# Copying the transposed u straight out of PSUM, and reordering it in the gate's fp32 matmul instead

## The chip, the cores and the metric

The kernel runs on one core of one Trainium2 chip. The metric is the device time of one launch in microseconds. The time before is 427.67 us, the median of three runs (427.49 to 428.02).

## What is computed

An image `x` of 16 batches, 32 x 32 places and 32 channels goes through three residual layers. The first is an upsampling and downsampling filter with a leaky ReLU; the second is causal self-attention over the 1024 places of a batch; the third is a mixture of 16 experts, and it is this one that the change touches:

```python
t = t + attention(layernorm(t))              # t: 16 batches x 1024 tokens x 32
u = layernorm(t)
logits = einsum('bsd,ed->bse', u, gate_w) + gate_b
probs = softmax(logits, axis=1)              # over the 1024 tokens of a batch
vals, idx = top_k(probs.transpose(0, 2, 1), 8)   # each expert takes 8 tokens of each batch
pooled = sum over the 8 tokens of u[token] * probs[token]
out = gelu([pooled, 1] @ weight1) @ weight2      # per expert
t[token] += out * probs[token]
```

## The kernel before

The 16 batches are worked through one after the other, and everything that concerns the gate is done for four batches at once (a group; G = 4 groups). The order of the work is a list written by hand, `EVENTS`, which every engine walks through: an engine executes the events that concern it and leaves the others out, so one list sets the order of each of the five queues. In the middle of the kernel the list interleaves stages of several batches (`STEP`); the last group's gate and the experts' work come in the order of `LAST` (L140 to L143).

The stages of the gate for group n are these. "uT" on TensorE (L973) turns the normalised tokens `u` with eight fp32 transposes into two PSUM banks of psA, 128 partitions (four batches times 32 channels) by 1024 tokens. "uT" on VectorE (L752) copies these 1024 columns into the SBUF tile `uT`. The columns come as (a, r, q) with a of 2, r of 4 and q of 128, and they are written as (a, q, r): VectorE reads PSUM in order and writes every fourth place of `uT` (16 bytes apart), four times 128 places for each half. After this a token stands at its own number. "logits" on TensorE (L976) waits for that copy and multiplies the block-diagonal gate matrix `gateT` (128 x 64) by the 1024 columns of `uT`, in two fp32 products of 512 columns. ScalarE then adds the bias and copies the 64 x 1024 logits to `lg` (L564), VectorE looks for the eight largest (L755, L759), ScalarE makes the exponential and the scaling (L568, L572), VectorE masks the rest (L764), and TensorE turns the weights back ("wT", L980), reading `xF_all` through `by_tile`, every fourth column as the stationary operand. "pool" (L983) and the experts ("hidden", "experts", "turned", "scatter") follow.

The program writes one product of fp32 operands; the trace shows two pairs of a weight load and a matmul for each, so the two products of a group are four MATMULs of 128 x 512 (a transpose is one pair).

The same tile `uT` is also called `att`: "proj" on VectorE (L720) writes into it before "mean" adds it to `t2_all`, and it waits until the last group's logits are in `lg` (L721). In front of the next group's `att` nothing else reads `uT`.

In the middle of the kernel "uT" is followed on VectorE by work on other batches ("low", "down", "shift", "score"), and on TensorE between "uT" and "logits" lie "down", "shift", "zV", "prob" and "score" of other batches. In `LAST` TensorE finds between ("uT", 3) and ("logits", 3) the event ("experts", 0): 32 small products of `hid` with `w2_sb` (L999).

Of the kernel before, what the change touches and what calls it, by code (L numbers as in the profile page):

```python
# [17 lines left out]
R = P // C  # L18
# [16 lines left out]
GE = GB * E_  # L35
# [5 lines left out]
BANK = 512  # L41
# [152 lines left out]
def hybrid_kernel(nc, x, bias, up_filter, dn_filter, Wq, Wk, Wv, gate_w, gate_b, weight1, weight2, out):  # L194
# [8 lines left out]
    with ExitStack() as ctx:  # L203
# [3 lines left out]
        def sem(name):  # L207
            return ctx.enter_context(nc.semaphore(name))
# [41 lines left out]
        uT = sb("uT", [P, S])  # L250
# [25 lines left out]
        gateT = sb("gateT", [P, GB, E_])  # L276
# [52 lines left out]
        a_filled, a_drained = sem("a_filled"), sem("a_drained")  # L329
# [251 lines left out]
        def _(dve):  # L581
# [19 lines left out]
            for e in EVENTS:  # L601
# [3 lines left out]
                s = slot(e) if e in A else None  # L605
                if name == "xT":
                    nc.vector.tensor_copy(xF_all[:, n, :], s).then_inc(a_drained, 1)
                    dve.wait_ge(a_drained, A[e] + 1)
                    for b in range(GB):
                        link(nc.vector.bn_stats(stats[:, :], xF_all[:, n, BC * b:BC * b + BC]))  # L610
                        ins = nc.vector.bn_aggr(mv[:, n, b, :], stats[:, :])
# [11 lines left out]
                elif name == "normalise":  # L623
                    dve.wait_ge(g_rstd, nth("gn_var", n))
                    for b in range(GB):
                        r = slice(BC * b, BC * b + BC)
                        ins = nc.vector.tensor_scalar(x_all[:, n, r], xF_all[:, n, r], gmean[:, n, b:b + 1], grstd[:, n, b:b + 1],
                                                      ALU.subtract, ALU.mult)
# [13 lines left out]
                elif name == "UU":  # L642
                    dve.wait_ge(fills_ready, 4)
                    dve.wait_ge(U_split, 2)
                    for r in range(R):
                        q = slice(C * r, C * r + C)
# [23 lines left out]
                elif name == "dnT":  # L670
# [4 lines left out]
                    for r in range(R):  # L675
                        ins = nc.vector.tensor_copy(DD[:, :, r:r + NS, r, :], D_parts[:, :, :, :])
# [13 lines left out]
                elif name == "split_z":  # L690
                    s = centred[:, :].rearrange("p (n c) -> p n c", c=C)
# [13 lines left out]
                elif name == "score":  # L705
                    if n >= 2:
                        dve.wait_ge(a_filled, A["shift", n - 2] + 1)
                    for m, at in packed(e[2]):
                        ins = nc.vector.tensor_reduce(negmax[:, n % 2, m - 1:m], s[:, at:at + P * m], X, ALU.max, negate=True)  # L709
# [40 lines left out]
                        dve.wait_ge(t2_rstd, 2 * G)  # L750
                        nc.vector.tensor_tensor(pair_of_u(e[2]), pair_of_u(e[2]), per_token(urstd[:, :]), ALU.mult).then_inc(u_ready, 1)
                elif name == "uT":  # L752
                    nc.vector.tensor_copy(uT[:, :].rearrange("p (a q r) -> p a r q", a=2, r=R),
                                          s.rearrange("p (a r q) -> p a r q", a=2, r=R)).then_inc(a_drained, 1)
                elif name == "logit_max":  # L755
                    dve.wait_ge(b_drained, BU["logits", n] + 1)
                    link(nc.vector.max(top8[:, :], lg[:, :]))
# [28 lines left out]
                elif name == "pool":  # L786
                    for b in range(GB):
                        ins = nc.vector.tensor_copy(pooled32[:, :, b], s[C * b:C * b + C, E_ * b:E_ * b + E_])
# [12 lines left out]
                elif name == "turned":  # L801
                    groups = range(PARTS[n][0] // GB, PARTS[n][1] // GB)
                    for g in groups:
                        ins = nc.vector.tensor_tensor(obd[:, g, :, :], s[0:GE, C * g:C * g + C].unsqueeze(1).broadcast_to([GE, GB, C]),
                                                      blocks(GB, C, GE, C_BDE), ALU.mult)
                    ins.then_inc(a_drained, 1)
                elif name == "scatter":
                    for a in range(2):
# [3 lines left out]
                        else:  # L812
                            dve.wait_ge(a_filled, A[e] + 1)
                        ins = nc.vector.tensor_tensor(x_all[:, n, :].rearrange("p (b k c) -> p k b c", b=GB, k=KT)[:, tiles],
                                                      s.rearrange("p (k b c) -> p k b c", b=GB, k=KT)[:, tiles],
                                                      t2_all[:, n, :].rearrange("p (b k c) -> p k b c", b=GB, k=KT)[:, tiles], ALU.add)
# [3 lines left out]
        def _(pe):  # L820
# [32 lines left out]
            for e in EVENTS:  # L853
# [4 lines left out]
                s = slot(e) if e in A or e in BU else None  # L858
                if name == "xT":
                    pe.wait_ge(x_loaded[n], 16)  # L860
                    ins = turn(s, lambda k: x_all[:, n, P * k:P * k + P], ident)
                elif name == "gn_mean":
                    pe.wait_ge(stats_ready, nth("xT", n))
                    ins = nc.tensor.matmul(s[:, 0:GB], cst[:, C_AVG:C_AVG + P], mv[:, n, :, 0], start=True, stop=True)
                elif name == "gn_var":
                    pe.wait_ge(a_drained, A["gn_mean", n] + 1)
                    ins = nc.tensor.matmul(s[:, 0:GB], cst[:, C_AVG:C_AVG + P], gvar[:, n, :], start=True, stop=True)
                elif name == "small" and n == 0:
# [3 lines left out]
                    ins = nc.tensor.matmul(s[:, BANK:BANK + E_], gw_sb[:, :, :], ident[0:E_, 0:E_], start=True, stop=True)  # L872
                elif name == "small" and n == 1:
                    pe.wait_ge(a_drained, A["small", 0] + 1)
                    nc.tensor.matmul(s[0:C, 0:C], A_sb[:, :], cst[0:C, C_Q:C_Q + C], start=True, stop=True)
                    ins = nc.tensor.matmul(s[:, BANK:BANK + C], cst[0:C, C_QREP:C_QREP + P], wvT[:, :], start=True, stop=True)
                elif name == "small":
                    pe.wait_ge(a_drained, A["small", 1] + 1)
                    ins = nc.tensor.matmul(s[:, 0:C], T1[:, :, :], cst[0:C, C_Q:C_Q + C], start=True, stop=True)
                elif name == "dnT":  # L880
                    pe.wait_ge(dn_toeplitz_loaded, 16)
                    rows = dnE.rearrange("p a t -> p (a t)")
                    for m in range(NS):
                        ins = nc.tensor.matmul(s[:, C * m:C * m + C], rows[:, 2 * W * (2 * m + 1):2 * W * (2 * m + 3)], ident[0:C, 0:C],
                                               start=True, stop=True)
# [18 lines left out]
                elif name == "tok":  # L904
# [3 lines left out]
                    for k in range(HB):  # L908
                        ins = nc.tensor.matmul(s[:, BC + P * k:BC + P * k + P], image_cols(n, k), cst[:, C_Q:C_Q + P], start=True, stop=True)
# [41 lines left out]
                elif name == "pv":  # L951

                    pe.wait_ge(b_drained, BU["zV", n] + 1)
                    waited = set()
                    for j in range(KT):
                        unit = next(u_ for u_ in range(NU) if KT - j in PACK[u_])
                        if unit not in waited:
                            waited.add(unit)
                            pe.wait_ge(*low_count(n, unit))
                        o, N = PLACE[j], P * (KT - j)  # L960
                        for part in range(2):
                            probs_j = Pp[:, n % 2, part, o:o + N].rearrange("p (t r q) -> p t r q", r=2, q=2 * C)
                            for odd in range(2):
                                rows = s[2 * C * odd:2 * C * odd + 2 * C, :].rearrange("p (r t q) -> p t r q", r=2, t=KT)[:, j:KT]
                                ins = nc.tensor.matmul(rows, zV[:, n % 3, j, :], probs_j[:, :, :, C * odd:C * odd + C],  # L965
                                                       start=j == 0 and part == 0, stop=j == KT - 1 and part == 1, skip_group_check=True)
                elif name == "proj":
                    pe.wait_ge(b_drained, BU["pv", GB * n + 2 * e[2] + 1] + 1)
                    for k in range(KT):
                        b, a, r = k // 4, k // 2 % 2, k % 2  # L970
                        at = S // 4 * r + P * a
                        ins = nc.tensor.matmul(s[:, P * k:P * k + 2 * C + 2], oT[:, 2 * e[2] + b, at:at + P], V2[:, :], start=True, stop=True)  # L972
                elif name == "uT":  # L973
                    pe.wait_ge(u_ready, 2 * n + 2)
                    ins = turn(s, lambda k: u[:, k, :], ident)
                elif name == "logits":  # L976
                    pe.wait_ge(a_drained, A["uT", n] + 1)
                    for i in range(2):
                        ins = nc.tensor.matmul(s[0:GE, BANK * i:BANK * i + BANK], gateT[:, :, :], uT[:, BANK * i:BANK * i + BANK], start=True, stop=True)  # L979
                elif name == "wT":  # L980
                    pe.wait_ge(route_ready, n + 1)
                    ins = turn(s, by_tile(xF_all[0:GE, n, :]), ident[0:GE, 0:GE], GE)
                elif name == "pool":  # L983
                    pe.wait_ge(a_drained, A["wT", n] + 1)
                    for k in range(KT):
                        ins = nc.tensor.matmul(s[:, 0:GE], u[:, k, :], wT[:, k, :], start=k == 0, stop=k == KT - 1)
                elif name == "hidden":
                    first, last = PARTS[n]
                    if n == 0:
                        pe.wait_ge(w1_split, 2)  # L990
                    pe.wait_ge(pooled_split, 2 * (last // GB))
                    for x_ in range(E_):
                        ins = nc.tensor.matmul(s[:, B * x_ + first:B * x_ + last], w1_parts[:, x_, :], pooled[:, x_, first:last], start=True, stop=True)
                elif name == "experts":
                    first, last = PARTS[n]
                    pe.wait_ge(b_drained, BU["hidden", n] + 1)
                    sv = s[0:C, 0:B * E_].rearrange("p (b e) -> p e b", b=B)[:, :, first:last]
                    for x_ in range(E_):
                        ins = nc.tensor.matmul(sv[:, x_, :], w2_sb[:, x_, :], hid[:, x_, first:last], start=True, stop=True)  # L999
                elif name == "turned":  # L1000
                    pe.wait_ge(a_drained, A["experts", n] + 1)
                    for g in range(PARTS[n][0] // GB, PARTS[n][1] // GB):
                        ins = nc.tensor.transpose(s[0:GE, C * g:C * g + C], o2[:, GB * g:GB * g + GB, :], ident[0:C, 0:C])
                elif name == "scatter":
                    pe.wait_ge(a_drained, A["turned", n // (G - 1)] + 1)
                    tile = by_tile(xF_all[0:GE, n, :])
                    for k in range(KT):
                        ins = nc.tensor.matmul(s[:, P * k:P * k + P], tile(k), obd[:, n, :, :], start=True, stop=True)  # L1008
                        if k == R - 1:
                            ins.then_inc(half_filled, 1)  # L1010
                else:
                    continue
# [26 lines left out]
```

## Time and profile before

| | |
|---|---|
| median of three runs | 427.67 us |
| profiled execution, its own time | 429.69 us |
| its span on the core | 427.8 us |
| TensorE matmuls, busy | 356.7 us, 83% |
| VectorE busy | 323.8 us, 76% |
| ScalarE busy | 257.0 us, 60% |
| GpSimd busy | 238.3 us, 56% |
| granted TensorE clock, mean | 0.892 |

The profile is of one execution. Its span is the time from the first to the last instruction on the core; 1.89 us of its own time lie outside that span. Busy shares are means over the whole span, and the stages differ: up to about 340 us the four engines all work at once, from 390 us on only TensorE, VectorE and ScalarE take turns, at half of TensorE's clock. A group of instructions is named by its line, engine, and output <- inputs, and a MATMUL names the moving operand first, the stationary operand second. "idle before <- X" is the time for which the engine stood still before the group, and X is what ended it. A matmul's own duration includes the way through the array, which overlaps the next one; the pace of a series is read from the starts, or from the length of the whole series over its count.

### The profile page before, as it was taken

To read this page: it belongs to the slowest core of one execution; us is meant where nothing else is said; L and a number is where in the kernel's file an instruction comes from. 1 tells how busy PE (TensorE), PEld (TensorE's weight loads), DVE (VectorE), ACT (ScalarE), POOL (GpSimd) and SP (SyncE) were. 2 spreads that over 40 slices of the span, in tenths; PEclk is the share of its full clock that TensorE was granted. 3 is DMA by queue.
4 is the path that set the end of the run, shared out by engine and by line. 5 is a ranking of instruction groups with operands and counts; after the bars stand their busy time and mean duration, and the time that the engine had idled before them with its cause. 6 is when DMAs were issued, how large, how long until landed. Compare 5 with 4: busy or idle time off the path is not lost.

```text
span 427.8 us, 7761 instructions
## 1 busy us (share of the span) xinstructions
PE 356.7 (83%) x3022; PEld 267.0 (62%) x3022; DVE 323.8 (76%) x551; ACT 257.0 (60%) x342; POOL 238.3 (56%) x138
## 2 busy tenths in 40 slices
PE   1199899999999997989988979898788697854995
PEld 1088777677778584748766847486654345443785
DVE  3878957887778778987787789777979888773631
ACT  0122424788998867589766675997485856811500
POOL 5405543485895996774755967747558735132000
PEclk9999979999999998999998989999898886855555
DMA  4700000000000000000000000000410000000122
GB/s 110 180 1 2 0 2 2 2 3 1 3 2 2 2 2 1 2 2 0 2 2 2 0 3 0 2 2 2 90 13 2 1 0 2 2 0 0 51 73 75
DMA packets 16432, 6.82 MB, mean 16 GB/s; under 512 B 6479, under 2 KB 16269, under 8 KB 16397
## 3 DMA queue, kind: packets, MB, share of 16 engines
q1 hardware_dynamic: 13680, 5.68, 5.7%
q10 hardware_dynamic: 2717, 0.66, 0.9%
q8 instruction: 24, 0.39, 0.4%
q14 instruction: 11, 0.09, 0.1%
HBM read 4.16 MB, written 2.11 MB: 15 GB/s over the span
## 4 chain that ended last, share of the span: by engine, by line
PE 55%; DVE 18%; issue 9%; ACT 9%; DMA 3%; POOL 2%; SPq 1%; POOLq 1%; ACTq 1%; DVEq 0%
PE psB L839 10%; PE psA L839 9%; PE psB L965 5%; PE psB L947 5%; PE psA L932 4%; DVE negmax L709 4%; PE psA L1008 4%; PE psA L972 3%; ACT e L552 3%; ACT Pp L553 3%; PE psB L979 3%; DVE Pp L376 2%; PE psA L829 2%; DVE t_all L734 2%; PE psA L925 2%
## 5 line engine op out<-in xcount | busy, mean ns | idle before, releaser
L376 POOL TENSOR_TENSOR Pp<-e,Pp 128x1024 f16<-128x1024 f32 x45 | 99.1, 2203 | 30.8 <-ACT Pp L553 30.6
L709 DVE TENSOR_REDUCE negmax<-psA 128x1 f32<-128x512 f32 (+7 forms) x128 | 91.0, 750 | 21.2 <-PE psA L935 20.8
L552 ACT ACTIVATE e<-psB 128x1024 f32<-128x1024 f32 (+1 forms) x80 | 76.1, 951 | 11.0 <-PE psB L947 8.6
L553 ACT ACTIVATE Pp<-psB 128x1024 f16<-128x1024 f32 (+1 forms) x80 | 76.7, 958 | 0.0
L839 PE MATMUL psB<-xin,UU 128*128 128x224 f16 (+1 forms) x480 | 60.1, 287 | 2.1 <-ACT oT L557 1.8
L947 PE MATMUL psB<-yQ,zK 128*128 128x512 f16 (+1 forms) x192 | 51.6, 347 | 7.4 <-ACT Pp L553 4.6
L839 PE MATMUL psA<-y,DD 128*128 128x224 f16 (+1 forms) x480 | 55.2, 273 | 1.5 <-DVE negmax L709 1.5
L839 PEld LDWEIGHTS psB<-xin,UU 128*128 128x128 f16 x480 | 49.1, 103 | 11.0 <-ACT oT L557 2.1
L932 PE MATMUL psA<-zK,yQ 128*128 128x512 f16 x192 | 47.7, 337 | 7.2 <-DVE tF L682 5.7
L839 PEld LDWEIGHTS psA<-y,DD 128*128 128x128 f16 x480 | 46.6, 98 | 7.2 <-DVE negmax L709 1.9
L441 POOL TENSOR_TENSOR zrstd<-zrstd,power 128x8 f32<-128x8 f32 x16 | 30.8, 1924 | 30.4 <-DVE zrstd L689 30.1
L463 POOL TENSOR_TENSOR y<-y 128x1024 f16<-128x1024 f32 x16 | 37.9, 2371 | 17.2 <-ACT y L518 17.2
L965 PE MATMUL psB<-Pp,zV 128*64 128x128 f16 (+7 forms) x512 | 38.7, 299 | 8.1 <-DVE Pp L376 7.9
L376 DVE TENSOR_TENSOR Pp<-e,Pp 128x1024 f16<-128x1024 f32 (+1 forms) x35 | 40.9, 1176 | 0.9 <-ACT Pp L553 0.7
L965 PEld LDWEIGHTS psB<-Pp,zV 128*64 128x64 f16 x512 | 24.6, 114 | 24.9 <-DVE Pp L376 12.1
L515 ACT ACTIVATE y<-psB 128x1024 f16<-128x1024 f32 x16 | 16.4, 1023 | 33.4 <-PE psB L839 33.4
L947 PEld LDWEIGHTS psB<-yQ,zK 128*128 128x128 f16 x192 | 17.5, 102 | 24.4 <-ACT Pp L553 9.1
L441 POOL TENSOR_TENSOR urstd<-urstd,power 128x16 f32<-128x16 f32 x8 | 23.2, 2894 | 12.9 <-DVE urstd L748 12.9
L704 DVE TENSOR_TENSOR yQ<-psA,yQ 64x1024 f16<-64x1024 f32 x16 | 19.6, 1228 | 13.6 <-ACT yQ L541 13.5
L932 PEld LDWEIGHTS psA<-zK,yQ 128*128 128x128 f16 x192 | 17.2, 101 | 20.3 <-DVE tF L682 6.3
L950 PE MATMUL psB<-ident_b,mask_b 128*128 128x128 bf16 x128 | 29.2, 228 | 0.0
L471 POOL COPY z<-z 128x512 f16<-128x512 f16 x16 | 12.8, 803 | 25.3 <-DVE z L700 25.3
(154 smaller groups left out, 626.4 us busy)
## 6 DMA issues: line engine op xcount, KB each, us to landing
x_all<-in_x_dram SPq DMA_DIRECT2D x4, 512.0 KB, 4.7
out_dram<-x_all SPq DMA_DIRECT2D x8, 256.0 KB, 2.3
y<-in_L_ffn_weight_dram SPq DMA_DIRECT2D x3, 256.0 KB, 4.2
yQ<-rows SPq DMA_DIRECT2D x32, 2.0 KB
Pp<-filter_tables ACTq DMA_DIRECT2D x4, 121.9 KB, 3.1
cst<-shape_constants SPq DMA_DIRECT2D x1, 326.5 KB, 4.3
xin<-in_L_ffn_weight_dram SPq DMA_DIRECT2D x1, 256.0 KB, 4.8
Pp<-filter_tables ACTq DMA_DIRECT2D x1, 120.0 KB, 3.3
```

The source lines that it names most:

```text
L376: return engine.tensor_tensor(Pp[:, n % 2, 1, o:o + N], e32[:, (NU * n + i) % 3, 0:N], Pp[:, n % 2, 0, o:o + N], ALU.subtract)
L441: return nc.gpsimd.tensor_tensor(v, v, power[:, 0:1].broadcast_to([P, n]), ALU.pow)
L463: nc.gpsimd.tensor_tensor(low, y32[:, :], high, ALU.subtract).then_inc(y_ready, 1)
L552: nc.scalar.activation(e32[:, m % 3, 0:N], slot(e)[:, 0:N], ACT.Exp)
L553: nc.scalar.activation(Pp[:, n % 2, 0, UOFF[e[2]]:UOFF[e[2]] + N], slot(e)[:, 0:N], ACT.Exp).then_inc(b_drained, 1)
L704: nc.vector.tensor_tensor(v, s[2 * C:P, :], v, ALU.subtract).then_inc(a_drained, 1)
L709: ins = nc.vector.tensor_reduce(negmax[:, n % 2, m - 1:m], s[:, at:at + P * m], X, ALU.max, negate=True)
L839: ins = nc.tensor.matmul(within(out_cols, -shift), m, within(v, shift), start=i == 0, stop=i == len(matrices) - 1)
L932: ins = nc.tensor.matmul(s[:, lo:hi], yQ[:, n % 3, P * (m - 1):P * m], zK[:, n % 3, lo - at:hi - at], start=True, stop=not diagonal)
L947: ins = nc.tensor.matmul(s[:, lo:hi], zK[:, n % 3, P * j:P * j + P], yQ[:, n % 3, P * j + lo - at:P * j + hi - at], start=True, stop=not d ...
L950: ins = nc.tensor.matmul(s[:, lo:lo + P], mask_b[:, :], ident_b[:, :], start=False, stop=True)
L965: ins = nc.tensor.matmul(rows, zV[:, n % 3, j, :], probs_j[:, :, :, C * odd:C * odd + C], start=j == 0 and part == 0, stop=j == KT - 1 and ...
```

## The change

VectorE copies the 1024 columns of PSUM into `uT` in the order in which they stand, (a, r, q). Each of the two products of "logits" then reads its 512 columns of `uT` in the order (q, r): r is the inner step. So the output columns stand in the order of the tokens as before, and `lg` and all behind it is unchanged. Going by the access pattern, one column and the next are 128 fp32 values (512 bytes) apart in groups of four, and each group of four begins one place (4 bytes) behind the last; "four places apart", as the change is called in words, is the spacing of the writes that it removes. The number of instructions, their sizes, the waits and the order of the events stay the same.

```diff
                 elif name == "uT":
-                    nc.vector.tensor_copy(uT[:, :].rearrange("p (a q r) -> p a r q", a=2, r=R),
-                                          s.rearrange("p (a r q) -> p a r q", a=2, r=R)).then_inc(a_drained, 1)
+                    nc.vector.tensor_copy(uT[:, :], s).then_inc(a_drained, 1)
...
                 elif name == "logits":
                     pe.wait_ge(a_drained, A["uT", n] + 1)
                     for i in range(2):
-                        ins = nc.tensor.matmul(s[0:GE, BANK * i:BANK * i + BANK], gateT[:, :, :], uT[:, BANK * i:BANK * i + BANK], start=True, stop=True)
+                        ins = nc.tensor.matmul(s[0:GE, BANK * i:BANK * i + BANK], gateT[:, :, :], uT[:, BANK * i:BANK * i + BANK].rearrange("p (r q) -> p q r", r=R), start=True, stop=True)
```

## Rows read from the trace of the kernel before

**Rows 1.** Table by stage: stretch, busy us (instructions) per engine, PEclk, DMA share, GB/s.

```profile
60.00:176.00 116.00, 110.34 (x1041) 83.28 (x1040) 89.53 (x151) 89.74 (x122) 84.36 (x49) 0.99 0.01 2
...
390.00:427.80 37.80, 30.76 (x184) 26.42 (x184) 14.75 (x30) 6.29 (x7) 0.00 (x0) 0.50 0.20 56
```

**Rows 2.** The chain that ended last, in time: start us, us, engine, line.

```profile
176.96 3.46 PE psA L839 x30
181.79 1.86 PE psB L979 x4
185.85 1.02 ACT zK L531
...
267.41 1.86 PE psB L979 x4
...
341.98 3.68 PE psB L979 x4
...
392.27 1.97 DVE uT L753
394.38 3.64 PE psB L979 x4
```

**Rows 3.** The lines L753 and L607: VectorE copies, ns min/median/max, first and last start.

```profile
L753 DVE COPY uT<-psA x4: 1958/2006/2014, 176.8 to 392.3; 128x1024 f32<-128x1024 f32 x4
L607 DVE COPY xF_all<-psA x4: 1215/1222/1226, 7.6 to 41.9; 128x1024 f32<-128x1024 f32 x4
```

**Rows 4.** Timeline of the end: start, us, engine, line, operation, [idle before <- releaser].

```profile
392.17 1.88 PE L999 MATMUL psA<-hid,xin 128*32 128x12 f32 x32
392.27 1.96 DVE L753 COPY uT<-psA 128x1024 f32<-128x1024 f32 x1 [2.12 <-PE psA L829]
394.09 0.35 DVE L799 TENSOR_TENSOR o<-psA,w2bias 32x192 f32<-32x192 f32 x1
...
394.38 3.64 PE L979 MATMUL psB<-uT,gateT 128*64 128x512 f32 x4 [0.33 <-DVE uT L753]
```

**Rows 5.** Timeline about the first of the four copies.

```profile
176.82 2.01 DVE L753 COPY uT<-psA 128x1024 f32<-128x1024 f32 x1
...
181.34 0.41 DVE L682 SCALAR_TENSOR_TENSOR tF<-psA,xF_all 128x256 f32<-128x256 f32 x1
...
181.72 1.93 PE L979 MATMUL psB<-uT,gateT 128*64 128x512 f32 x4
...
183.58 0.55 PE L932 MATMUL psA<-zK,yQ 128*128 128x512 f16 x2
...
184.34 1.29 DVE L709 TENSOR_REDUCE negmax<-psA 128x1 f32<-128x896 f32 x2 [1.48 <-PE psA L935]
```

**Rows 6.** Timeline about the third copy.

```profile
338.04 2.00 DVE L753 COPY uT<-psA 128x1024 f32<-128x1024 f32 x1 [0.48 <-PE psA L829]
...
341.98 3.68 PE L979 MATMUL psB<-uT,gateT 128*64 128x512 f32 x4 [1.50 <-ACT Pp L553]
...
346.35 2.48 DVE L709 TENSOR_REDUCE negmax<-psA 128x1 f32<-128x896 f32 x4 [1.14 <-PE psA L935]
```

**Rows 7.** Table by stretch, columns as in rows 1: the clock during the gate's products.

```profile
181.00:184.00 3.00, 3.00 (x14) 1.07 (x13) 1.82 (x5) 2.75 (x4) 2.85 (x2) 1.00 0.00 1
341.00:346.00 5.00, 4.02 (x7) 0.98 (x8) 4.17 (x5) 1.23 (x3) 2.12 (x1) 0.54 0.00 1
394.00:398.00 4.00, 3.67 (x6) 0.79 (x6) 0.43 (x2) 0.00 (x0) 0.00 (x0) 0.50 0.00 0
```

**Rows 8.** Timeline: transposes with a stationary operand in order and with a spaced one.

```profile
175.25 1.04 PE L829 MATMUL psA<-cst,u 128*128 128x128 f32 x8
...
206.62 1.17 PE L829 MATMUL psA<-cst,xF_all 64*128 64x64 f32 x8
...
207.73 0.39 PE L947 MATMUL psB<-yQ,zK 128*128 128x512 f16 x1
```

**Rows 9.** The chain in time, at half clock: the same transposes with the spaced operand.

```profile
361.38 1.15 PE psA L829 x8
```

## The prediction

> **What bounds the kernel now.** I read the table by stage first. From 60 to 176 us TensorE is busy for 110.34 of 116.00 us at a granted clock of 0.99, and it stays the fullest engine up to about 340 us; in the last 37.80 us it is busy for 30.76, at clock 0.50 [rows 1]. So the middle is paced by TensorE, with VectorE close behind, and the end is a chain in which the engines take turns. The reader should see that the change takes time from VectorE and can only add time to TensorE.
>
> Next I read the chain that ended last, in order of time, for the four groups. The copy L753 stands in it once, at the end (392.27, 1.97 us). In the middle the chain passes beside it: near the first group it goes from the convolution L839 (176.96) through the gate's products L979 (181.79, 1.86 us) to ScalarE's zK (185.85), and at the later place through L979 again (341.98, 3.68 us) [rows 2]. So there are four copies of which one counts, and four sets of products which all count. Two early sets, at 181.79 and 267.41, take 1.86 us each; the clock at the first was 1.00 and the second repeats it. The sets at 341.98 and 394.38 ran at 0.54 and 0.50, that is at 1.2 GHz [rows 7].
>
> **The copy.** What is left is a plain copy of 128 x 1024 fp32 from PSUM to SBUF. The trace of before holds exactly this form: L607, 1222 ns. The reordering copy takes 2006 ns, so each copy becomes 0.78 us shorter (the last one, 1958 ns, becomes 0.74 us shorter) [rows 3]. The sum over four is 3.1 us of VectorE.
>
> How much of it is on the path? At the end, TensorE does the 32 small products of the experts, 392.17 to 394.05, while VectorE copies, 392.27 to 394.23; the gate's products begin at 394.38, after an idle time of 0.33 us that the copy ended [rows 4]. With the copy done at 393.49, the experts' products end last, and the gate can begin at 394.05 plus almost nothing. So the cover of those 1.88 us leaves a gain of 0.33 us out of 0.74. What is late next is TensorE itself. The experts' addition L799 can't begin before the experts' products end, and it begins at 394.09 already [rows 4], so nothing else moves up. All that follows the gate hangs on L979 (the chain goes from the copy into it [rows 2]) and moves with it.
>
> In the middle I take the copy's gain as zero. After the copy at 176.82, VectorE has L376 and then L682 (181.34); these would come some 0.7 us earlier. But TensorE is busy without a gap from the products at 181.72 into L932 at 183.58, so no wait for VectorE stands there, and the next thing VectorE does after that, L709 at 184.34, waited 1.48 us for TensorE already [rows 5]. The 0.78 us become a longer wait there. The group at 338.04 is the same: the gate waited for ScalarE (1.50 us, Pp L553), not for the copy, and VectorE then waited 1.14 us for TensorE before L709 at 346.35 [rows 6]. If the cover were gone in all three places the gain would be 3 x 0.78 = 2.3 us more; that is a rival below.
>
> **The gate's products.** No row of before shows a moving operand read with its columns 512 bytes apart, so this cost has to be bounded. Before: four MATMULs from 181.72 to 183.58 [rows 5], which is 465 ns for each 512 columns or 0.91 ns per column at full clock; at half clock 3.64 / 4 = 910 ns, 1.78 ns per column [rows 4].
>
> The lower bound is no cost: the instruction needs a new fp32 value only every 0.91 ns, which a read may still keep up with. A gain is excluded, since the counts and the sizes stay the same, and an instruction that read in order already can't be read faster.
>
> The nearest row on TensorE is the weight load of "wT", which reads 128 fp32 values 16 bytes apart. Eight of its transposes take from 206.62 to 207.73, 139 ns each, at full clock; eight transposes whose operand is read in order, and which stream twice as many columns, take 1.04 us or 130 ns each [rows 8]. At half clock the spaced ones take 1.15 us, 144 ns each [rows 9]. Half the work in no less time, and a pace that hardly moves when the clock halves: I read this as a limit in the read and not in the array, 139 / 128 = 1.09 ns for each fp32 value that is read apart from its neighbours. Applied to the moving operand, 512 x 1.09 = 556 ns in place of 465 at full clock, so 91 ns more for each MATMUL, 0.36 us for a set of four and 0.73 us for the two sets at full clock. At half clock 556 ns lie below the 910 ns that the array takes, and nothing is added.
>
> The farther row is VectorE's own spaced write: (2006 - 1222) / 1024 = 0.77 ns more for each value [rows 3]. Put upon the measured plain pace of 1.09 ns/value as the cost of going from line to line, it is 1.86 ns, or 952 ns for 512 columns: 487 ns more for a MATMUL at full clock, 42 ns more at half clock. That is 8 x 0.487 + 8 x 0.042 = 4.2 us. The upper bound is the limit of 1.09 ns with every column read twice, once for each of two sweeps of the array: 1112 ns, or 647 more at full and 202 more at half clock, 8 x 0.647 + 8 x 0.202 = 6.8 us. I take 1.09 ns once, since it is the row on the same engine and of the same type of data.
>
> The rows of the spaced write and of the spaced weight load both show a cost for 16 bytes already [rows 3, 8]. The Trainium skill, in "SBUF — State Buffer" (the note on SBUF cachelines), says that reads are at full rate as long as at least two fall on the same line of 16 bytes, and that a stride of up to four fp32 values is free; past that every access pays. The new reads are far past that and speak against the change; the old write at 16 bytes cost 0.77 ns a value in this trace, so here the trace does not bear out that four are free. The page gives no price, so the sum stays as it is.
>
> **The sum.** Products +0.73, copy at the end -0.33, copies in the middle 0: +0.40 us. The profiled execution took 429.69 us with a span of 427.8, 2.02 us above the median of 427.67 us; the change in the span carries over to the median: 428.07, rounded to 428.1 us.
>
> **Why the products' cost is passed on.** TensorE goes from L979 straight into L932 at 183.58, whose scores VectorE was waiting for (1.48 us) [rows 5], and the chain leads on from L979 to zK [rows 2]. There is no slack behind the products in the middle that would take up 0.36 us.
>
> **The rivals.** The measurement of this kernel can tell about 0.2% (0.86 us) from no change: below 426.8 is faster, over 428.5 slower.
>
> Rival A: the moving read keeps up, because a column is wanted only every 0.91 ns. For it speaks that the needed pace is only a sixth below the 1.09 ns limit and that this port need not have the weight port's limit; against it the spaced weight loads [rows 8]. Only the end's 0.33 us are left: 427.3 us, not to be told from no change.
>
> Rival B, slower: going from line to line costs TensorE's moving port more than its weight port, from the 952 ns to the 1112 ns above, or four values 512 bytes apart fall on the same part of the memory. Its place is the eight MATMULs at full clock. The price is 4.2 - 0.33 = +3.9 us, 431.5 us, up to 6.8 - 0.33 = +6.5, 434.1 us. It decides once it costs 1.19 us (0.86 + 0.33), which is 149 ns per MATMUL at full clock: 614 ns, 1.20 ns per column. For it speaks VectorE's 0.77 ns [rows 3]; against it, that TensorE's weight port took 1.09 ns in all.
>
> Rival C, faster: VectorE's 0.78 us reach the path in some of the three places of the middle as well, since VectorE there is nearly as full as TensorE (89.53 of 116.00 us [rows 1]). All three with rival A give 427.67 - 0.33 - 2.3 = 425.0 us, one or two of them 426 to 426.5. Against it are the waits of 1.48 and 1.14 us in which VectorE stood still right afterwards [rows 5, 6].
>
> That the change doesn't do what it says (the copy stays at 2.0 us) is nearly excluded by L607, the same form [rows 3]: 428.4 us then.
>
> **How the numbers follow.** The forecast (428.1) has 0.36, rival A (427.3) 0.24, rival B (431.5 to 434.1) 0.28, rival C (425.0 to 426.5) 0.11, the last one 0.01. The range of 426.5 to 432.0 holds the forecast, A, the cheaper part of B (0.17 of 0.28) and the edge of C (0.03): 0.80. Faster: C, 0.11. Slower: B and a tenth of the forecast, whose 91 ns per MATMUL need only be 149: 0.32. Same: 0.57.
>
> **What would show it right or wrong.** In the profile after, L753 should stand at 1222 ns four times. At the end L979's idle time before should fall from 0.33 us to near 0, ended by L999 and not by the copy. The four MATMULs of L979 near 181 us should take about 2.2 us from start to start of what follows, where it was 1.86; those near 342 and 394 us should be unchanged at 3.6 us. VectorE's wait before L709 near 184 us should grow from 1.48 us to over 2. The forecast is wrong if the sets at half clock also become longer (then the read is slower than 1.78 ns per column, rival B), or if the span shortens before 390 us (rival C), or if TensorE's clock falls in another stretch because its work has moved.

## The result

The changed kernel takes 432.57 us (median of 14 runs, 428.9 to 434.5), where the kernel before took 427.94 us in the 14 runs beside it (425.44 to 432.74). The ratio is 1.010 with an interval of 1.0065 to 1.0135, that is 2.8 to 5.8 us slower. A second series gave 1.0067 (1.0035 to 1.0099). The single executions of one and the same kernel lie over 7 us apart, so only ratios over many runs are compared below, and lengths of single operations where possible. The ratios leave out executions over 1.5% above the fastest of their kernel, which are two of the kernel before and none of the changed one; with all 14 of each the means are 428.8 and 432.1 us, 3.4 us apart. The changed kernel's times fall into two clusters, six from 428.9 to 430.33 us and eight from 432.52 to 434.5 us, and its median lies at the edge of the upper one.

The prediction was 428.1 us with a range of 426.5 to 432.0: the median lies above the range. What happened is in the direction of rival B: the spaced read costs far more than the row that I had chosen says, though less than B's cheapest price.

The profile after is of an execution of 429.86 us with a span of 428.0 us, one of the quicker ones. First the line of the gate's products in the kernel before, and then the two lines that the change touches, from the changed kernel (ns min/median/max, first and last start); the copy is to be held against [rows 3]:

```profile
L979 PE MATMUL psB<-uT,gateT x16: 592/852/1117, 181.7 to 397.0; 128*64 128x512 f32 x16
```

```profile
L978 PE MATMUL psB<-uT,gateT x16: 1047/1048/1116, 181.2 to 397.2; 128*64 128x512 f32 x16
L753 DVE COPY uT<-psA x4: 1212/1224/1225, 176.3 to 392.8; 128x1024 f32<-128x1024 f32 x4
```

The copy is at the predicted length. The MATMUL, which has moved up by one line, has nearly one length in all four groups, at full clock and at half, where it had from 592 to 1117 ns before. Next the chain that ended last, in time, to be held against [rows 2]:

```profile
181.31 3.61 PE psB L978 x4
187.12 1.02 ACT zK L531
...
266.15 3.60 PE psB L978 x4
...
344.04 3.72 PE psB L978 x4
...
394.56 3.66 PE psB L978 x4
```

The first two sets take 3.61 and 3.60 us where they took 1.86; the last two stay where they were (3.68 and 3.64 before). The timeline about the first set, to be held against [rows 5]:

```profile
176.35 1.21 DVE L753 COPY uT<-psA 128x1024 f32<-128x1024 f32 x1
...
181.24 3.68 PE L978 MATMUL psB<-uT,gateT 128*64 128x512 f32 x4
...
184.85 0.55 PE L931 MATMUL psA<-zK,yQ 128*128 128x512 f16 x2
...
185.61 1.29 DVE L709 TENSOR_REDUCE negmax<-psA 128x1 f32<-128x896 f32 x2 [3.55 <-PE psA L934]
```

From 181.24 to 184.85 four MATMULs pass, 902 ns each or 1.76 ns per column (465 ns and 0.91 before), and VectorE's wait for TensorE before L709 grows from 1.48 to 3.55 us: 1.74 us of that is TensorE's. The other 0.33 us are what is left of the copy's 0.80, for L376 right behind the copy took 3.14 us where it took 2.73 before. The timeline of the end, against [rows 4]:

```profile
392.68 1.88 PE L998 MATMUL psA<-hid,xin 128*32 128x12 f32 x32
392.79 1.23 DVE L753 COPY uT<-psA 128x1024 f32<-128x1024 f32 x1 [2.12 <-PE psA L828]
394.49 3.73 PE L978 MATMUL psB<-uT,gateT 128*64 128x512 f32 x4
394.60 0.35 DVE L798 TENSOR_TENSOR o<-psA,w2bias 32x192 f32<-32x192 f32 x1 [0.59 <-PE psA L998]
```

The idle time of 0.33 us before the gate's products is gone, and they follow the experts' products.

Why, then, is the span only 0.2 us longer than before? The table by stretch of the kernel before and, behind it, of the changed kernel:

```profile
176.00:262.00 86.00, 77.38 (x699) 57.70 (x697) 71.32 (x108) 62.46 (x84) 58.28 (x31) 0.96 0.01 1
```

```profile
176.00:262.00 86.00, 76.54 (x703) 56.15 (x704) 70.95 (x110) 61.86 (x83) 57.30 (x30) 1.00 0.01 1
```

In the profiled execution of after the clock stayed at 1.00 through this stretch, where it was at 0.96 before. From one set of products to the next it took 84.84 us (181.31 to 266.15) against 85.62 before, although it holds 1.74 us more of work. From there to the third set it took 77.89 us (266.15 to 344.04) against 74.57, and from the third to the last 50.52 (to 394.56) against 52.40, at a mean clock of 0.74 against 0.70. So the clock's fall in other places than before shifts single stretches by as much as the reads do. Another execution with the spaced read, of the kernel read_spaced below (434.77 us), shows the other side: from its first set to its second it took 3.87 us longer than the changed kernel's did, at 0.94,

```profile
180.65:269.36 88.71, 80.53 (x697) 57.92 (x698) 71.20 (x108) 62.00 (x83) 57.75 (x31) 0.94 0.01 1
```

and a second profile of the changed kernel (432.59 us) took 88.53 us there, also at 0.94. Whether the spaced read makes such falls of the clock more frequent can't be told from so few profiles. The two profiled executions of before and after alone would have hidden the loss that 14 runs show.

### The profile page after: what moved, and what is told of

Its sections match the earlier page's. It is cut to its first block, busy times and chain, and to the rows that moved or that the text cites. A ratio compares the mean times of both kernels' runs of the same rounds, so it can differ in the third digit from the quotient of the medians.

```text
span 428.0 us, 7761 instructions
## 1 busy us (share of the span) xinstructions
PE 355.0 (83%) x3022; PEld 262.3 (61%) x3022; DVE 320.6 (75%) x551; ACT 256.9 (60%) x342; POOL 237.5 (55%) x138
## 4 chain that ended last, share of the span: by engine, by line
PE 56%; DVE 18%; ACT 9%; issue 8%; DMA 3%; POOL 2%; SPq 1%; POOLq 1%; ACTq 1%; DVEq 0%
PE psB L838 10%; PE psA L838 9%; PE psB L964 6%; PE psB L946 5%; DVE negmax L709 4%; PE psA L931 4%; PE psA L1007 4%; PE psB L978 3%; ACT Pp L553 3%; ACT e L552 3%; PE psA L971 3%; PE psA L828 2%; DVE Pp L376 2%; DVE t_all L734 2%; PE psA L985 2%
## 5 line engine op out<-in xcount | busy, mean ns | idle before, releaser
L376 POOL TENSOR_TENSOR Pp<-e,Pp 128x1024 f16<-128x1024 f32 x45 | 100.5, 2236 | 31.3 <-ACT Pp L553 31.1
L709 DVE TENSOR_REDUCE negmax<-psA 128x1 f32<-128x512 f32 (+7 forms) x128 | 90.8, 749 | 24.8 <-PE psA L934 24.6
L838 PE MATMUL psB<-xin,UU 128*128 128x224 f16 (+1 forms) x480 | 58.9, 284 | 2.0 <-ACT oT L557 1.8
L946 PE MATMUL psB<-yQ,zK 128*128 128x512 f16 (+1 forms) x192 | 50.7, 342 | 8.7 <-ACT Pp L553 4.6
L463 POOL TENSOR_TENSOR y<-y 128x1024 f16<-128x1024 f32 x16 | 36.9, 2309 | 16.6 <-ACT y L518 16.6
L376 DVE TENSOR_TENSOR Pp<-e,Pp 128x1024 f16<-128x1024 f32 (+1 forms) x35 | 40.0, 1151 | 0.9 <-ACT Pp L553 0.7
L471 POOL COPY z<-z 128x512 f16<-128x512 f16 x16 | 11.8, 740 | 26.7 <-DVE z L700 26.7
```

The source lines that it names most:

```text
L376: return engine.tensor_tensor(Pp[:, n % 2, 1, o:o + N], e32[:, (NU * n + i) % 3, 0:N], Pp[:, n % 2, 0, o:o + N], ALU.subtract)
L463: nc.gpsimd.tensor_tensor(low, y32[:, :], high, ALU.subtract).then_inc(y_ready, 1)
L838: ins = nc.tensor.matmul(within(out_cols, -shift), m, within(v, shift), start=i == 0, stop=i == len(matrices) - 1)
L946: ins = nc.tensor.matmul(s[:, lo:hi], zK[:, n % 3, P * j:P * j + P], yQ[:, n % 3, P * j + lo - at:P * j + hi - at], start=True, stop=not d ...
```

## The experiments

**Each half of the change by itself.** The first kernel has only the plain copy:

```diff
-                    nc.vector.tensor_copy(uT[:, :].rearrange("p (a q r) -> p a r q", a=2, r=R),
-                                          s.rearrange("p (a r q) -> p a r q", a=2, r=R)).then_inc(a_drained, 1)
+                    nc.vector.tensor_copy(uT[:, :], s).then_inc(a_drained, 1)
```

> Only the copy is changed: PSUM is copied in order, and the products read it in order too, so the logits stand in the order (a, r, q) and the weights go to other tokens than the reference's. Theory R (the products pay for the spaced read, the copy's gain is hidden in the middle): L753 at 1.22 us, the four MATMULs of the gate 1.86 us at full clock as before, the end 0.33 us earlier, total 0.3 us below before. Rival V (VectorE's time counts in the middle): three more times 0.78 us, up to 2.6 us below before. Rival K (the change's loss is TensorE's clock falling in other stretches because work has moved): a shift of some us up or down that no length of an instruction explains.

Measured: ratio 0.9993 (0.9961 to 1.0024), 427.81 us against 428.5 us. The first chain row and the copy's line:

```profile
181.92 1.86 PE psB L978 x4
```

```profile
L753 DVE COPY uT<-psA x4: 1215/1220/1225, 176.9 to 395.7; 128x1024 f32<-128x1024 f32 x4
```

3.1 us less of VectorE's work is worth between 1.7 us of gain and 1.0 us of loss; the expected 0.3 us lie within this, and the 2.6 us of rival V (ratio 0.994) don't. The copy ends no wait of another engine in this trace, as forecast for the middle; the time alone would leave room for one of the three places (0.33 + 0.78 = 1.1 us).

The second kernel keeps the reordering copy and has only the spaced read:

```diff
-                        ins = nc.tensor.matmul(s[0:GE, BANK * i:BANK * i + BANK], gateT[:, :, :], uT[:, BANK * i:BANK * i + BANK], start=True, stop=True)
+                        ins = nc.tensor.matmul(s[0:GE, BANK * i:BANK * i + BANK], gateT[:, :, :], uT[:, BANK * i:BANK * i + BANK].rearrange("p (r q) -> p q r", r=R), start=True, stop=True)
```

> Only the read is changed: the reordering copy of 2.0 us stays, and the products read their columns 512 bytes apart on top of it, so the logits stand in another order than the reference's. Theory R: four MATMULs take 3.6 us at full clock in place of 1.86, twice; at half clock 3.64 us as before; total 3.5 us above before, 0.8% . Rival K: below 1 us above before, or a spread over several us.

Measured: ratio 1.0123 (1.0083 to 1.0164), 3.6 to 7.0 us slower; 3.5 us stood just below that. The chain:

```profile
180.65 3.61 PE psB L979 x4
...
269.36 3.61 PE psB L979 x4
...
346.40 3.68 PE psB L979 x4
...
397.41 1.97 DVE uT L753
399.52 3.70 PE psB L979 x4
```

So the read alone carries the whole loss, at the same 3.61 us per set. Why the ratio lies even above the 3.5 us isn't shown; the length of the sets doesn't explain it, and the 3.87 us of the stretch above are of the right size.

**The same time added to TensorE without any spaced read.** In the kernel before, the gate's products of groups 0 and 1 are issued twice:

```diff
-                    for i in range(2):
+                    for i in (0, 1, 0, 1) if n <= 1 else (0, 1):
```

> The kernel before, with the gate's products of groups 0 and 1 (full clock) each issued twice; the second overwrites the first with the same values. TensorE has 2 x 1.86 us more at the place where the changed kernel has 2 x 1.74 us more, and nothing is read spaced. Theory R (time added to TensorE there is passed on whole): 3.7 us above before, 0.9%, within the interval the same as read_spaced (1.2%). Rival S (part of it is taken up by waits behind it): below 2 us.

Measured: ratio 1.0078 (1.0045 to 1.0111), 1.9 to 4.8 us slower. The chain:

```profile
179.87 3.58 PE psB L979 x8
...
266.92 3.58 PE psB L979 x8
```

Each set is 3.58 us long, all but the length of the spaced one, and the loss is the changed kernel's within the intervals. In the same series the changed kernel itself was run again:

> The changed kernel itself once more, beside the other three on one chip. Theory R (8 MATMULs of the gate at full clock take 0.90 us in place of 0.465: 3.5 us, less 0.33 us at the end): 3.2 us above before, 0.75%. Rival K (what the change costs is mostly the clock's fall elsewhere): away from this by more than the interval, and with another sign on another chip.

Measured: ratio 1.0067 (1.0035 to 1.0099), 1.5 to 4.2 us slower. The 3.2 us of theory R lie in this interval and in that of the first series (2.8 to 5.8 us). Time on TensorE at this place is passed on, at least half of it (1.9 of 3.4 us) by the interval, and no further property of the spaced read is needed. Rival K, by which most of the loss is the clock's fall elsewhere, isn't needed for the ratios either, though the clock does move single executions by as much (84.84 and 88.5 us for the same stretch above).

**Which spacing costs.** One kernel reads each of the eight products in an order of its own, with the reordering copy kept:

```diff
+ORDERS = ((("p (m t) -> p t m", dict(t=2)), ("p (m t) -> p t m", dict(t=4))),
+          (("p (h m t) -> p m h t", dict(h=2, t=2)), ("p (h m t) -> p m h t", dict(h=2, t=4))),
...
                     for i in range(2):
-                        ins = nc.tensor.matmul(s[0:GE, BANK * i:BANK * i + BANK], gateT[:, :, :], uT[:, BANK * i:BANK * i + BANK], start=True, stop=True)
+                        how, size = ORDERS[n][i]
+                        columns = uT[:, BANK * i:BANK * i + BANK].rearrange(how, **size)
+                        ins = nc.tensor.matmul(s[0:GE, BANK * i:BANK * i + BANK], gateT[:, :, :], columns, start=True, stop=True)
```

> The reordering copy stays; each of the eight products of the gate reads its 512 columns in an order of its own, so the logits stand in other orders than the reference's. Group 0 (full clock): step of 2 places (8 bytes), step of 4 (16 bytes). Group 1 (full clock): 2 neighbours and then 256 places on, 4 neighbours and then 256 places on. Groups 2 and 3 (half clock): steps of 2 and 4; 2 neighbours, and the changed kernel's order. Theory L (what costs is leaving a line of 16 bytes at every column, 1.76 ns each): step 4 at 900 ns for a MATMUL, step 2 between 465 and 900 ns, 2 neighbours the same as step 2, 4 neighbours 465 ns. Rival D (distance counts, not lines): step 4 is at or near 465 ns and only far jumps cost, so both neighbour orders cost too. At half clock all stay near 910 ns by either.

Measured, the chain of this kernel:

```profile
180.55 2.84 PE psB L985 x4
...
267.07 1.91 PE psB L985 x4
...
342.42 2.91 PE psB L985 x4
```

and MATMULs of the first set, the two with a step of 2 places, and then the last, with a step of 4 (ns min/median/max, starts):

```profile
L985 PE MATMUL psB<-uT,gateT x2: 610/636/662, 180.5 to 181.0; 128*64 128x512 f32 x2
```

```profile
L985 PE MATMUL psB<-uT,gateT x1: 1079/1079/1079, 182.3 to 182.3; 128*64 128x512 f32 x1
```

A single MATMUL's length includes its way through the array; in the kernel before 592 ns (643 for the first of a set) stand for a mean pace of 465, in the changed one 1047 for 902. With 8 bytes from one column to the next the two are 662 and 610 ns, about 20 ns more, so next to nothing is paid; with 16 bytes it is 1079. The set with both is 2.84 us long, two at about 0.48 and two at about 0.94. The set with two or four neighbours followed by a jump of 256 places (1024 bytes) is 1.91 us long: the far jump is free as long as two columns stand side by side. The third set ran at full clock in this execution (in the table its stretch has 1.00) and repeats the first:

```profile
342.40:345.30 2.90, 2.88 (x5) 0.50 (x6) 2.87 (x5) 0.00 (x0) 2.57 (x1) 1.00 0.00 1
```

Theory L was right in kind; the room that it left for a price at the step of 2 is hardly used. Rival D falls. A second kernel of the same make takes wider steps:

> As spacings_a, with other orders (the logits stand in other orders than the reference's). Group 0 (full clock): steps of 8 and of 32 places (32 and 128 bytes). Group 1 (full clock): the changed kernel's order (512 bytes), then in order. Groups 2 and 3: the same four again. Theory L: steps of 8, of 32 and of 128 places cost the same as the step of 4, 900 ns a MATMUL, since each leaves its line of 16 bytes; in order 465 ns. Rival D: the farther the dearer. At half clock all 910 ns.

```profile
181.79 3.68 PE psB L985 x4
...
269.95 2.73 PE psB L985 x4
...
398.01 3.66 PE psB L985 x4
```

Steps of 32 and 128 bytes together take 3.68 us, 920 ns each, the changed kernel's order with an in-order product 2.73 us, and at half clock all is at 3.66. Between 16 and 512 bytes the distance makes no difference worth the name (940, 920 and 902 ns). A step of 3 places, and neighbours that lie on two lines, were not tried: that it is the line of 16 bytes that counts, and not the distance from one column to the next, fits all orders here but isn't shown apart.

This agrees with one half of what the Trainium skill says in "SBUF — State Buffer" (the note on SBUF cachelines), that a line of 16 bytes needs two accesses to run at full rate, and not with the other: there a stride of up to four fp32 values is called free, and four places, a new line for every column, cost about twice the time here (0.94 against 0.48 us).

**The changed kernel mended.** Two neighbouring places are read before each jump, and the outputs go to their places in PSUM:

```diff
-                        ins = nc.tensor.matmul(s[0:GE, BANK * i:BANK * i + BANK], gateT[:, :, :], uT[:, BANK * i:BANK * i + BANK].rearrange("p (r q) -> p q r", r=R), start=True, stop=True)
+                        view = s[0:GE, BANK * i:BANK * i + BANK].rearrange("p (q t r) -> p q r t", t=2, r=R)
+                        columns = uT[:, BANK * i:BANK * i + BANK].rearrange("p (r q t) -> p q r t", r=R, t=2)
+                        ins = nc.tensor.matmul(view, gateT[:, :, :], columns, start=True, stop=True)
```

> The changed kernel, but each product reads two neighbouring places before it jumps 512 bytes, and its outputs are written to PSUM four places apart in pairs, so that the logits stand in the order of the tokens. Theory L (leaving the 16-byte line at every column costs, two columns to a line are free): the four MATMULs take 1.9 us at full clock, total 0.3 us below before. Rival W: the spaced writes into PSUM cost as much as the spaced reads did, 3.6 us a set, total as the changed kernel.

Measured: ratio 0.9969 (0.9941 to 0.9997), the set at

```profile
180.25 1.91 PE psB L980 x4
```

The whole loss is gone with the same jump of 512 bytes left in place. The gain of 0.33 us at the end lies in the interval (0.1 to 2.5 us), which barely leaves out no change. The set is 0.05 us longer than before, so the writes into PSUM, four places apart, cost next to nothing. The same was asked of the turns of u, with the copy plain and the products in order:

```diff
-                    ins = turn(s, lambda k: u[:, k, :], ident)
+                    w = s.rearrange("p (a q r) -> p a r q", a=2, r=R)
+                    for k in range(KT):
+                        ins = nc.tensor.transpose(w[:, k // R, k % R, :], u[:, k, :], ident)
```

> The reordering moved to the turns of u in place of the copy: each of the eight fp32 transposes writes its 128 columns four places apart in PSUM; the copy is plain and the products read in order. If the spaced write into PSUM costs TensorE nothing, the turns stay at 1.04 us for eight at full clock and 1.94 us at half clock, and the total is as copy_plain, 0.3 us below before. Rival W: a spaced write costs as much per column as the spaced read (0.9 us per 512): 0.3 us or more on each set, and the copy's gain is gone.

Measured: ratio 0.9991 (0.9965 to 1.0017), as copy_plain, and the turns at

```profile
L976 PE MATMUL psA<-cst,u x32: 272/273/445, 174.9 to 394.8; 128*128 128x128 f32 x32
```

as in the trace of the kernel before:

```profile
L829 PE MATMUL psA<-cst,u x32: 272/273/446, 175.2 to 391.8; 128*128 128x128 f32 x32
```

Rival W falls in both kernels.

**Nothing reordered at all.** Softmax and the choice of the eight largest don't ask for an order of the tokens, so the order (a, r, q) can be kept through to the scatter. Beside the plain copy this takes

```diff
-                w = v.rearrange("p (a q r) -> p a r q", a=2, r=R)
-                return lambda k: w[:, k // R, k % R, :]
+                return lambda k: v[:, P * k:P * k + P]
```

> Nothing is reordered: plain copy, products in order, and the turns of the weights (wT) and the scatter take their 128 columns side by side instead of every fourth. The softmax and the choice of eight don't depend on the order of the tokens. Theory R: the copy's end gains 0.33 us; the eight turns of a group fall from 139 ns to below 130 ns each, below 0.1 us a group at full clock; scatter at half clock 244 ns each as before; total 0.4 to 1.0 us below before. Rival V: up to 2.6 us below.

> The kernel without any reordering once more, beside the changed one. By the lengths measured in its first profile: turns of the weights 0.64 us in place of 1.10 at full clock, twice; scatter 3.76 us in place of 4.08 for 16 at half clock, four times; the end of the copy 0.33: about 2.5 us below before, 0.6%; and 5.7 us below the changed kernel.

Measured: ratio 0.9907 (0.9873 to 0.994), 424.15 us, and 0.9911 (0.9877 to 0.9945), 424.24 us, in a second series. This beats both kernels. In the first expectation I had forecast at most 1.0 us under theory R; it was 4 us. The chain of before has, for a turn of the weights and for the last scatter,

```profile
206.69 1.10 PE psA L829 x8
...
420.33 4.08 PE psA L1008 x16
```

and the chain of no_reorder, to be held against this and [rows 9]:

```profile
206.97 0.64 PE psA L827 x8
...
361.87 1.04 PE psA L827 x8
...
410.01 3.71 PE psA L1006 x16
417.58 3.76 PE psA L1006 x16
```

The turns of the weights fall from 138 to 80 ns each at full clock, where I had expected "below 130". The scatter's pairs at half clock fall from 255 ns (4.08 us for 16) to 235: the spaced weight load was not hidden behind the array at half clock either. The last kernel changes this line alone and keeps the reordering copy:

> The kernel before with its reordering copy, but the weight loads of wT and scatter take 128 columns side by side, so the weights go to other tokens than the reference's. It is the half of no_reorder that doesn't touch the copy. Theory R: no_reorder's gain comes from here: turns 2 x 0.46 us at full clock, scatter 4 x 0.32 us at half clock, wT at half clock 0.1, about 2.3 us below before, 0.5%; with the copy's 0.33 it makes up no_reorder. Rival V (the copy's 0.78 us count in the middle once TensorE has less to do): close to before.

Measured: ratio 0.9923 (0.9896 to 0.9949), 2.2 to 4.5 us faster. So most of no_reorder's gain is the weight loads' and not the copy's, and the rival V falls again.

The expected 2.3 us are below the 4.0 us of no_reorder because they take the scatter as it is at half clock. In the profile of no_reorder the clock rose before the first 32 pairs of the scatter, and it did so in the profile of copy_plain as well, which loads its weights spaced and is no faster than before. The clock (last but two of the columns) over the first 1.80 us of those pairs, copy_plain first:

```profile
401.80:403.60 1.80, 1.80 (x8) 1.80 (x8) 1.66 (x4) 1.62 (x3) 0.00 (x0) 1.00 0.04 9
```

```profile
398.80:400.60 1.80, 1.80 (x16) 1.80 (x17) 1.68 (x4) 1.61 (x3) 0.00 (x0) 1.00 0.03 9
```

In the same time at full clock 16 matmuls pass with the loads in order, and 8 with the spaced ones. The whole series in the kernel before (all at half clock), in copy_plain and in no_reorder:

```profile
399.18 7.80 PE L1008 MATMUL psA<-obd,xF_all 64*128 64x128 f32 x32 [0.86 <-DVE obd L804]
```

```profile
401.80 7.80 PE L1007 MATMUL psA<-obd,xF_all 64*128 64x128 f32 x32 [0.86 <-DVE obd L803]
```

```profile
398.78 5.46 PE L1006 MATMUL psA<-obd,xF_all 64*128 64x128 f32 x32 [0.86 <-DVE obd L803]
```

So the spaced loads take 7.80 us whether the clock is up or not, while the loads in order use the full clock where it is granted. From the start of this series to the next turns of the weights it is 7.60 us before (399.18 to 406.78) and 5.62 us in no_reorder (398.78 to 404.40), 2.0 us less; the chain goes through the series before, and past it, through ScalarE and VectorE, in no_reorder. With 0.92 us for two sets of turns at full clock, 0.2 for those at half and 0.64 for the last 32 pairs (20 ns each) that is 3.7 us, and with the copy's 0.33 it is the 4.0 us measured. It is a sum for executions in which the clock rises there, as in all three profiles with the loads in order; how often it does wasn't counted.

## Why the prediction failed

**What bounds the kernel, and the copy.** Right. The copy took 1.22 us, and its 3.1 us gave nothing that can be told from no change (copy_plain 0.9993, within 0.4%), and the path doesn't go through it in the middle. At the end, the 0.33 us of idle time went and the gate's products followed the experts', as forecast.

**The gate's products: the step that failed is the price of the spaced read at full clock.** The sum had 512 x 1.09 = 556 ns for a MATMUL, 91 ns more than before; measured are 902 ns, 437 more. Eight of them are 3.5 us in place of 0.73. With the 0.33 us taken off, this is 3.2 us, 0.75%, inside both intervals. On 427.67 us it would give 430.8 us, inside the stated range, and the second series had its median at 430.40 us; that the first one's lies at 432.57 is this price and, beyond it, the share of its executions in the upper cluster, which the prediction had no term for and which no run explains. The 1.09 ns came from the weight load of wT [rows 8], on the same engine but another port. Two things were wrong with that. A moving column of fp32 takes 0.91 ns in order, while a stationary one takes at most 80 / 128 = 0.63 ns (no_reorder), so the loads' price was that of a faster stream. And I set the row of the spaced load against turns that stream 128 columns (130 ns), where the loads were not what took the time; against the pace in order, 80 ns, the spaced load costs 1.7 times. Both figures hold the first and last turn of a series; inside it the starts in the traces are 120 ns apart with the spaced load and about 62 with the load in order, 1.9 times. The moving read costs 1.94 times. A ratio would have come near: 465 x 1.7 is 790 ns, +2.6 us, and by 1.9 it is 880 ns, +3.3 us. But the row for it, 80 ns, came only from no_reorder; the trace of before didn't have it.

**Half clock.** Right, and by little: 902 ns lie just below the 910 ns of a MATMUL in order there. The sets at half clock are 3.72 and 3.66 us where they were 3.68 and 3.64. The limit is one of time and not of TensorE's cycles, for a spaced MATMUL has 1047 ns at full clock and at half.

**The bounds.** They held, but the working of two of them was wrong. The farther row, VectorE's spaced write, gave 952 ns per MATMUL, 4.2 us in all, and the upper bound of two reads for every column 1112 ns. Measured is 902. I gave the nearer row 0.36 and rival B 0.28, and ended the range at 432.0, near the lower end of B's span of 431.5 to 434.1. The farther row put VectorE's 0.77 ns on 1.09 ns as "the measured plain pace"; but 1.09 is the pace of the spaced load, which holds a price for the spacing already. On the plain 0.91 ns it is 1.68 ns, 860 ns for a MATMUL and +3.2 us, the nearest of all to what was measured, though from another engine and a write. And the reason of the upper bound, one read for each of two sweeps, counts twice: the two sweeps are the two MATMULs of a product in the trace, and the sum has both already.

**Passed on.** Right: products_twice adds 1.72 us of ordinary products at each of the two places and loses 1.9 to 4.8 us, which holds the 3.4 us in full but doesn't exclude that a part was taken up.

**The resolution.** I took 0.2% for what can be told from no change, from three runs that lay within 0.53 us. Over 14 runs the same kernel spreads from 425.44 to 432.74 us, and the intervals are 0.3% wide to either side. That is why rival A, with 0.3 us, could not have been told from no change in any case.

**Rivals.** A falls (902 ns, not 465). B came true in its condition (902 ns are far over its 614) and not in its size: its price began at 952 ns and 431.5 us. Of its two reasons, that four values 512 bytes apart fall on the same part of the memory is out, since a step of 16 bytes costs as much and pairs 512 bytes apart cost nothing. C with two or all three places falls with copy_plain (at most 1.7 us of gain, where they ask for 1.9 and 2.7); one place isn't excluded by the time. The Trainium skill's rule against the change, cited in the prediction without a price, pointed the right way.

## What to carry to other kernels

A reordering that costs VectorE a spaced write isn't made free by giving it to TensorE: an fp32 moving operand whose every column is on a line of 16 bytes of its own runs at about half pace at full clock, and two neighbours before each jump are enough to avoid this. PSUM writes of matmuls four places apart cost next to nothing here. Before moving a reordering, ask whether anything behind it needs the order: here nothing did, and leaving it out made the kernel 0.9% faster, most of it from the weight loads. And price an unseen access by the ratio that the nearest row shows against its own undisturbed pace, not by its absolute time; if there is no row for that pace, one small run gets it.

## What the hardware showed beyond that

The spaced read has a fixed time, 1.76 to 1.84 ns per fp32 column for steps of 16, 32, 128 and 512 bytes at full clock, and for 512 bytes no other at half clock. A spaced fp32 weight load costs even at half clock (255 against 235 ns for a pair of the scatter), although the array seemed to cover it, and it costs far more at full clock: 8 pairs in 1.80 us where 16 pass with the loads in order. So it also keeps the kernel from gaining anything when the clock rises.

The mean granted clock of one kernel differs between executions, and often its time with it: the kernel before took 425.95 us at 0.91 and 432.91 us at 0.881. It doesn't tell all: the changed kernel took 430.28 and 434.25 us, both at 0.9. A change of 0.75% can't be read from one profiled execution of each kernel; the lengths of the single operations can.
